# Edge batches scaled ahead of the last two curves of a slot, first used a slot later, with a group of scatters behind every fifth batch

## The reference

```
xn = layernorm(x)
x  = x + gnn(xn, src, dst, edge_weight, ...) + mix(xn, ...)

gnn:  msgs = edge_vals[:, None] * x[edge_src]            # gather rows, scale by weight
      agg  = segment_sum(msgs, edge_dst, num_segments=N) # add at the target node
      ... two dense layers with batch norms
mix:  for i in range(4):                                 # DEPTH
        h = layernorm(x); x = x + linear_attn(h, Wq[i], Wk[i], Wv[i], Wo[i], bo[i])
        h = layernorm(x); x = x + gelu(h @ W1[i] + b1[i]) @ W2[i] + b2[i]
```

## Time and profile before

| | us |
|---|---|
| median of the runs | 5966.48 |
| profiled execution, its own time | 5967.55 |
| its span | 5965.8 |
| TensorE busy | 5235.8 (88%) |
| VectorE busy | 3348.4 (56%) |
| ScalarE busy | 2919.6 (49%) |
| GpSimd busy | 3921.9 (66%) |

### The profile page before, as it was taken

How to read it: one execution, slowest core, us unless ns; L and a number is a source line. 1 busy time by engine, 2 the same in 40 slices (tenths; PEclk the granted TensorE clock), 3 DMA queues, 4 the chain that set the end, 5 groups by cost and what they waited for, 6 DMA issues and landing times. The chain is left out here.

```text
span 5965.8 us, 89987 instructions
## 1 busy us (share of the span) xinstructions
PE 5235.8 (88%) x25856; PEld 4415.7 (74%) x25856; DVE 3348.4 (56%) x8788; ACT 2919.6 (49%) x7114; POOL 3921.9 (66%) x6674
## 2 busy tenths in 40 slices
PE   5579998999989999899868999996777877877899
PEld 2468887888878888788756888884556666666788
DVE  8667775444545555433325555555657777776641
ACT  6345554555555555555434333333445555555444
POOL 1677787777667666777747777775447777777000
PEclk8799999999999999999988999996789999999999
DMA  2322112114333333334454222213223333335300
GB/s 68 91 76 52 50 48 61 47 46 114 102 109 101 103 97 101 110 109 113 104 93 123 57 60 54 61 40 99 77 70 103 103 105 105 103 103 96 96 27 33
DMA packets 378210, 493.21 MB, mean 83 GB/s; under 512 B 97665, under 2 KB 315641, under 8 KB 375289
## 3 DMA queue, kind: packets, MB, share of 16 engines
q0 software_dynamic: 135008, 236.92, 16.7%
q1 hardware_dynamic: 242712, 250.54, 14.3%
HBM read 385.16 MB, written 102.04 MB: 82 GB/s over the span
## 5 line engine op out<-in xcount | busy, mean ns | idle before, releaser
L305 POOL DMA_INDIRECT edges_g<-xn_rows,edges_idx x880 | 862.7, 980 | 389.0 <-issue 230.7
L2047 POOL DMA_INDIRECT messages_g<-h_rows,edges_record x880 | 842.7, 958 | 399.6 <-issue 230.9
L248 POOL DMA_INDIRECT sorted_dst<-edges_record,edges_place x784 | 802.3, 1023 | 364.6 <-issue 216.3
L248 POOL DMA_INDIRECT sorted_src<-edges_record,edges_place x784 | 770.0, 982 | 289.5 <-issue 213.8
L1224 PE MATMUL mixer_f_ps<-mixer_f_out,mixer_w 128*128 128x250 f32 x3200 | 754.4, 379 | 17.5 <-issue 16.3
L1235 PE MATMUL mixer_y_ps<-mixer_w,mixer_g 128*125 128x256 f32 x3200 | 724.4, 379 | 0.0
L277 POOL MEMSET edges_idle<- 128x96 f32 x3328 | 619.4, 186 | 144.3
L1224 PEld LDWEIGHTS mixer_f_ps<-mixer_f_out,mixer_w 128*128 128x128 f32 x3200 | 603.6, 192 | 87.4 <-issue 19.6
L1235 PEld LDWEIGHTS mixer_y_ps<-mixer_w,mixer_g 128*125 128x125 f32 x3200 | 593.4, 188 | 85.6
L2219 PE MATMUL messages_s_ps<-messages_g,messages_one 128*128 128x257 f32 x1760 | 457.3, 404 | 101.6 <-DVE messages_one L2130 95.4
L1381 ACT ACTIVATE mixer_g<-mixer_f_ps,mixer_b 128x250 f32<-128x250 f32 x800 | 330.3, 465 | 385.1 <-PE mixer_f_ps L1224 383.0
(11 more groups left out here) (543 smaller groups left out, 10432.6 us busy)
## 6 DMA issues: line engine op xcount, KB each, us to landing
mixer_q<-qT SPq DMA_DIRECT2D x100, 250.0 KB
mix_rows<-mixer_rows SPq DMA_DIRECT2D x100, 250.0 KB
qT<-mixer_qT SPq DMA_DIRECT2D x75, 250.0 KB, 3.0
mixer_rows<-mix_rows SPq DMA_DIRECT2D x75, 250.0 KB
edges_g<-xn_rows,edges_idx POOLq DMA_INDIRECT x880, 3.1
messages_g<-h_rows,edges_record POOLq DMA_INDIRECT x880
sorted_dst<-edges_record,edges_place POOLq DMA_INDIRECT x784
sorted_src<-edges_record,edges_place POOLq DMA_INDIRECT x784
```

Source lines behind the costliest of these rows:

```text
L248: self.nc.gpsimd.indirect_dma_start(self.orders[s][0], bass.IndirectOffsetOnAxis(self.place[s][:, j:j + 1], 0), self.record[s][:, j, :], N ...
L305: self.nc.gpsimd.indirect_dma_start(self.g[n % GR][:, j, 0:D], None, self.table_d, bass.IndirectOffsetOnAxis(self.idx[:, t:t + 1], 0)).the ...
L2047: self.nc.gpsimd.indirect_dma_start(self.g[n % GR][:, j, :], None, self.table_d, bass.IndirectOffsetOnAxis(self.idx[:, t:t + 1], 0)).then_inc(
```

## The change

In ScalarE's part of a slot, the batches of the next slot (`coming`) are scaled in this one: the first ahead of `curve(p, m, 2)`, the second ahead of `curve(p, m, 3)`. The first slot with a batch moves one turn on (`first`), which spreads 110 batches over 59 turns instead of 60. A group of scatters stands behind every fifth batch instead of every sixth: 21 groups, 168 scatters in the mixer, where there were 17 groups with 136. The message stage keeps its 80, and the experts' stage has 536 instead of 568.

```diff
                 for i in range(slots):
                     m, n = base + i, base + i - 1
                     forward, attend = i < NCH, p < LAYERS and i >= 1
+                    coming = list(work[i + 1])
...
                     if attend and i >= 2:
                         queries_kept(n - 1)
-                    for batch in work[i][1:]:
+                    for batch in coming[0:1]:
                         edges.act_scale(act, batch)
                     if forward:
                         curve(p, m, 2)
+                    for batch in coming[1:]:
+                        edges.act_scale(act, batch)
+                    if forward:
                         curve(p, m, 3)
                         act.preload_act_table_set("natural_log_exp_and_others")
...
                     if attend:
                         keys_raised(n)
                         queries_raised(n)
-                    for batch in work[i + 1][0:1]:
-                        edges.act_scale(act, batch)
-                    if attend:
                         keys_kept(n)
...
-    first, turns = NCH + 1 + 17, 3 * (NCH + 1) + NCH
+    first, turns = NCH + 1 + 18, 3 * (NCH + 1) + NCH
...
-    share_of = {n: 2 * FOUR for n in range(GR - 1, NB - GR, 6)}
+    share_of = {n: 2 * FOUR for n in range(GR - 1, NB - GR, 5)}
```

## The result

The changed kernel took 6018.89 us (median of 6 runs, 6013.37 to 6023.47), the kernel before 5966.31 beside it: ratio 1.0087, with a 95% interval of 1.0074 to 1.01. It is slower, as predicted, but by 53 us and not by 30, and it lies above the range. The profiled execution took 6012.79 us with a span of 6011.0, so 45.2 us more than the profiled one of before; I compare these two.

What follows compares the result with a forecast made beforehand. TensorE was taken to bound passes 1 to 3, GpSimd pass 4. Mixer +30 us and experts' stage +2 us made 5998.5 for the median; the forecast was 5996, range 5975 to 6006.

Steps and rivals of the forecast that it cites:

- First batch one slot later: Passes 2 and 3: 63 batches instead of 64, so pass 4 starts 4.7 us earlier; pass 4 gets one batch more.
- GpSimd's train: GpSimd's run of gathers and scatter groups in pass 4: last gather predicted 32.7 us later, at 3056.8.
- The end of pass 4: Last chunk's q load waits for batch 105, is issued at 3031, lands with the crowd at 3070; mixer +30 us.
- Scalings moved: ScalarE scales both next batches ahead of curve parts 2 and 3: costed at nothing in passes 2 and 3.
- the cover I named: ScalarE's 2.33 us wait ahead of curve part 3 leaves 0.97 us delay; lower_part needs the fourth curve only at its half.
- more is lost than GpSimd's time: Rival, 8%: late batches hold curves 2 and 3, stalling TensorE and lowering its clock; passes lose 10 to 20 us more, 6010.
- The groups: Scatter groups: 21 instead of 17; hidden in GpSimd's waits up to pass 3, two more unhidden in pass 4, 11.8 us each.
- The crowd: Blank batches gathering row 0 at pass 4's end keep DMA engines 97% busy; each takes 13.7 us to land instead of 2.8.
- The experts' stage: Earlier memset frees the tail's VectorE copy (-8.3 us) but holds one in mid-stage (+10.4 us): net +2 us.
- q is in time: Rival, 19%: the pause behind batch 104 lets the last chunk's q load through; mixer +23 us, time 5991.5.
- the scatters are hidden: Rival, 8% for faster: GpSimd's earlier waits absorb pass 4's 35.4 us of extra work; time 5953.5 if the memset is covered.

Runs made afterwards that it cites:

- experiment 3: Kernel before with only the first batch one turn later, 110 batches over 59 turns; ratio 1.0033 to the kernel before, mixer +10.5 us.
- experiment 12: Changed kernel with ScalarE's old order of scalings, keeping the later first batch and groups behind every fifth batch; ratio 1.0031 to the kernel before, mixer +22.9 us.
- experiment 5: Kernel before with the new order of ScalarE's scalings in the fourth pass only; ratio 1.0019 to the kernel before, mixer +20.3 us.
- 14: Kernel before with all groups ahead of pass 4, blank slots gathering different rows, and ScalarE's new order; ratio 0.9915 to the kernel before, mixer -39.4 us.
- experiment 2: Kernel before with only a group of scatters behind every fifth batch instead of every sixth; ratio 0.9998 to the kernel before, mixer -1.6 us.
- experiment 9: Kernel before with blank slots gathering 128 different rows and a group behind every fifth batch; ratio 0.9974 to the kernel before, mixer -12.8 us.
- experiment 10: Kernel before with its 17 groups at batches 4 to 60, all ahead of pass 4; ratio 0.9943 to the kernel before, mixer -32.6 us.
- 11: Kernel before with all 17 groups ahead of pass 4 and blank slots gathering different rows; ratio 0.9887 to the kernel before, mixer -51.5 us.
- 1: Changed kernel with a group of scatters behind every sixth batch again; ratio 1.0053 to the kernel before, mixer +30.2 us.
- 7: Kernel before with blank slots gathering 128 different rows instead of row 0; ratio 0.9909 to the kernel before, mixer -35.5 us.

## Why the prediction was wrong

The direction and the place were right, and the sum's +30 us for the mixer came to +50.2. Along the sum, two terms failed. The first is "First batch one slot later", counted as a gain of 4.7 us by the start of pass 4. Pass 4 began 4.8 us later instead (2489.11 for 2484.33), and GpSimd's train 9 us later than forecast (batch 69 at 2486.63, for 2470.5 + 11.8 - 4.7 = 2477.6); alone this part costs 10.5 us. The second is the landing of batch 105 in "The end of pass 4", counted as 13.8 us and measured as 20.0. By the experiments, the step "Scalings moved", costed at nothing, is 27.3 of the 50.2 us. Part of that the sum did hold, in another place: it lets the load of q wait for batch 105 to land, which only the new order asks for.

- *Scalings moved.* In passes 2 and 3 the slots kept 30.36 and 27.0 us, as predicted, so the cover I named is there. The boundary slot ahead of pass 4 grew by 6.4 us. Of these 1.6 come with the numbers at an unchanged clock (65.34, experiment 3), the rest with the lower clock (TensorE busy 55.19 us for 50.52); with these numbers the old order has 70.15 too (experiment 12), so the order is not shown to be the reason in the changed kernel. What I had wrong is pass 4. There a batch is asked for up to a slot sooner than it was: where GpSimd is late, ScalarE stands ahead of curve part 2 or 3 until it lands, and TensorE waits for the curve (40.1 us after, 22.8 in experiment 5, none before and none in 14). I had this as the rival "more is lost than GpSimd's time" at 8%, with the argument that a GpSimd that never waits sets the pace whatever TensorE loses. The pace up to the last gather is indeed GpSimd's: from the start of batch 69 it took 3065.97 - 2486.63 = 579.3 us after; before it was 3024.12 - 2470.5 = 553.6, and with two groups 577.2 were to be expected; experiment 12 has 580.1. But TensorE falls behind it, and what it is behind is paid after the last gather: 64.5 us to the last row finish, 31.9 in experiment 12. Before it was 58.2, of which 14.3 are the rest of the stall for q.
- *First batch later.* The end of pass 3 came at 2418.92 with a mixer that began 2.0 us earlier: +0.4 instead of -4.7. Experiment 3 shows where the gain goes. Its pass 2, with two batches less, ends 4.3 us earlier (after the first row finish); the boundary slot behind it takes 1.1 more, with fewer matmuls (219 for 234) at a clock of 0.87 instead of 0.95; pass 3, with one batch more, 3.0 more; and the boundary slot ahead of pass 4 1.6 more. For the changed kernel this is shown only up to the sum of these parts, +0.4 at the end of pass 3 and 6.8 after the boundary slot.
- *The groups.* Two more units in pass 4 came to 25.7 us of GpSimd's time (579.3 - 553.6) against my 25.6. So the last gather is 9.2 us later than predicted because the train starts 9 us later.
- *The end of pass 4.* Batch 105 starts at 3008.51, not 3000, and is scaled at 3028.52: 20.0 us from its first gather. I took 13.8, which is from one instruction's issue to its landing, and left out the 10 that GpSimd needs to issue the batch. The row finish on which the load of q hangs comes at 3045.81 instead of 3031; q is issued 18 us later and lands at 3085.70, not 3070. From there to the end were 44.8 us (predicted 43.9). So these 16 us run through to the end: 3130.5 for 3114. The crowd itself was as sized: in the window 3024 to 3064 the DMA engines are 97% busy at 84 GB/s.
- *The experts' stage.* As predicted: a VectorE copy is caught in mid-stage for 8.15 us and the one at the end is free, and from the last row finish to GpSimd's load behind the stage were 999.2 us before and are 1001.5: +2.3, predicted +2. That it agrees so closely is partly luck, for I had the copy held for 10.4 us. The rows, of VectorE and of GpSimd, after the earlier trace rows:

```profile
4067.76 8.15 DVE L3124 COPY experts_scores<-experts_row 125x4 f32<-125x4 f32 x1
...
4124.96 0.17 DVE L3124 COPY experts_scores<-experts_row 125x4 f32<-125x4 f32 x1
```

```profile
4062.68 10.62 POOL L283 MEMSET edges_acc<- 128x12593 f32 x1
...
4132.02 0.56 POOL L2041 DMA_DIRECT2D messages_bucket<-bucket_src  x1 [56.14 <-POOLq L88]
```

The rivals: q is in time with the groups and the old order (experiments 2 and 12), where the load goes out 1.9 us ahead of the first gather of batch 105 and 3.2 us behind it; its matmul needs it 35.8 us later or more. In the changed kernel, issued 40.7 us behind that gather, it took 3085.70 - 3049.17 = 36.5 us, and TensorE was there 16.5 us before it. That the scatters are hidden was false for pass 4 (experiment 9) and true for passes 2 and 3 (experiments 10 and 11).

The Trainium skill (DMA: Bandwidth & Descriptors, "Queues, rings and completion order") has a DMA engine go round its queues packet by packet. The 36.5 us in the crowd don't speak for q getting through by that; in which order the packets were served no run here shows.

## What to carry to other kernels

Where one engine is late, the place at which another one waits for it is a cost of its own: put the work that waits for a late transfer behind what the bound engine needs next, not ahead of it. Before a cost is added to a window with a long stall, ask whether the stall covers it; the same groups cost 0, 12, 20 and 23 us in the mixer (experiment 2, 12 against 3, after against 1, 9 against 7), depending on what else was late. And give padding different addresses: here that alone was worth 0.9%.

## What the runs showed of the hardware

- Gathers of one row are slow by the rows that they name: 0.51 us a packet on average in the crowd against 0.14 with 128 different rows, with more packets in the same time. The DMA engines are occupied 3.6 times as long by each.
- With the same order of instructions and the same idle time (14.5 and 14.4 us), the boundary slot was granted a mean clock of 0.95 in experiment 10 and 0.85 in 11 (a mix of the levels 1.2 and 2.4 GHz), and took 64.83 and 69.97 us.
- A VectorE copy of 125x4 that starts within a GpSimd memset of 10.6 us is held for 8.15 us, as before (8.47). In both it ends not with the memset but with the second of the conversions behind it: at 4075.91 for 4075.88, before at 4076.28 for 4076.25.
